# A triangle-update layer with a mixture of experts on one core: the second root ahead of the first logits, two PSUM banks dealt out anew, and two groups' weights turned before the second variance

## The reference, cut to what matters

```python
x = x + triangle(ln_c(x))         # x is (1, 128, 128, 32)
t = tokens(x)                     # 16384 tokens of 32 channels
t = t + moe(ln_t(t))

# triangle(Z)
z = layernorm(Z, ln1_w, ln1_b)
g = sigmoid(z @ gate_w.T + gate_b)
left, right = split((z @ lrp_w.T + lrp_b) * mask * g)
tri = einsum('bikc,bjkc->bijc', left, right)
go = sigmoid(tri @ og_w.T + og_b)
tri + go * (layernorm(tri, ln2_w, ln2_b) @ op_w.T + out_bias)

# moe(x): 8 experts, the best 2 of each token
probs = softmax(x @ router_w + router_b)
top_p, top_i = top_k(probs, 2);  top_p = top_p / sum(top_p)
out = sum over the two of top_p * (x @ expert_w[e] + expert_b[e])
```

## Time and profile before

| | us |
|---|---|
| median of 3 runs | 144.69 (143.39 to 145.44) |
| the profiled execution, its own time | 144.41 |
| its span | 142.6 |
| PE busy in the span | 123.1 (86%) |
| DVE busy | 103.6 (73%) |
| ACT busy | 76.9 (54%) |
| POOL busy | 75.7 (53%) |

### The profile page before, as it was taken

How to read it: one execution, slowest core, us unless ns; L and a number is a source line. 1 busy time by engine, 2 the same in 40 slices (tenths; PEclk the granted TensorE clock), 3 DMA queues, 4 the chain that set the end, 5 groups by cost and what they waited for, 6 DMA issues and landing times. The chain is left out here.

```text
span 142.6 us, 2140 instructions
## 1 busy us (share of the span) xinstructions
PE 123.1 (86%) x708; PEld 53.8 (38%) x711; DVE 103.6 (73%) x173; ACT 76.9 (54%) x136; POOL 75.7 (53%) x73
## 2 busy tenths in 40 slices
PE   5999788999999699889799899695899669989970
PEld 2425145767679565344134443123121111212210
DVE  0096948787774699999918994462978995989951
ACT  4168473565413359898853349858256454474400
POOL 6001033799900089989930173063552974869970
PEclk9999999999999999999999999999559996999999
DMA  4997000000000000000000899987188978871112
GB/s 90 321 350 320 0 0 5 0 0 2 0 5 0 0 2 0 0 5 0 0 0 9 186 208 205 210 187 170 26 202 202 215 182 197 199 283 74 74 74 78
DMA packets 6171, 14.55 MB, mean 102 GB/s; under 512 B 1392, under 2 KB 1648, under 8 KB 6160
## 3 DMA queue, kind: packets, MB, share of 16 engines
q1 hardware_dynamic: 6160, 14.41, 38.1%
HBM read 3.85 MB, written 2.10 MB: 42 GB/s over the span
## 5 line engine op out<-in xcount | busy, mean ns | idle before, releaser
L429 POOL TENSOR_TENSOR work<-work,late_sb 128x512 f32<-128x512 f32 x12 | 15.0, 1274 | 9.7 <-ACT work L526 9.7
L627 ACT ACTIVATE wcopy<-ps 128x512 f32<-128x512 f32 x24 | 13.6, 597 | 9.1 <-PE ps L1024 9.0
L791 PE MATMUL ps<-w1m,xk 64*128 64x256 f32 x128 | 16.2, 391 | 0.8 <-DVE xk L1103 0.3
L1024 PE MATMUL ps<-w3F,selb 32*128 32x512 bf16 x64 | 12.0, 412 | 4.0 <-DVE prod L1306 2.7
L441 POOL TENSOR_TENSOR work<-tri,stats 128x512 f32<-128x512 f32 x8 | 8.8, 1114 | 11.6 <-DVE stats L1172 11.4
L526 ACT ACTIVATE work<-ps 128x512 f32<-128x512 f32 x16 | 9.6, 597 | 9.0 <-PE ps L791 9.0
L491 POOL TENSOR_TENSOR prod<-wcopy,lr 128x512 f32<-128x512 f32 x6 | 8.3, 1405 | 11.3 <-ACT wcopy L627 8.6
L791 PEld LDWEIGHTS ps<-w1m,xk 64*128 64x128 f32 x128 | 11.6, 186 | 5.5 <-DVE lr L1118 2.4
L1118 DVE TENSOR_TENSOR lr<-ps,work 128x512 f32<-128x512 f32 x16 | 10.6, 687 | 2.5 <-POOL work L429 2.5
L1089 DVE TENSOR_SCALAR xk<-ps,head_sb 128x512 f32<-128x512 f32 x8 | 6.4, 798 | 7.4 <-ACT triF L510 7.2
L1024 PEld LDWEIGHTS ps<-w3F,selb 32*128 32x128 bf16 x64 | 3.0, 93 | 20.4 <-issue 6.6
(11 more groups left out here) (136 smaller groups left out, 257.2 us busy)
## 6 DMA issues: line engine op xcount, KB each, us to landing
lr<-triF SPq DMA_DIRECT2D x32, 128.0 KB, 2.3
xi<-in_x_F SPq DMA_DIRECT2D x8, 256.0 KB, 4.6
tri<-triF SPq DMA_DIRECT2D x16, 128.0 KB, 2.4
xk<-triF SPq DMA_DIRECT2D x16, 128.0 KB, 2.3
out<-xi SPq DMA_DIRECT2D x8, 256.0 KB, 2.1
late_sb<-in_late SPq DMA_DIRECT2D x1, 914.0 KB, 7.6
choice_sb<-in_choice SPq DMA_DIRECT2D x1, 336.5 KB, 7.8
early_sb<-in_early SPq DMA_DIRECT2D x1, 257.0 KB, 5.5
```

Source lines behind the costliest of these rows:

```text
L429: pool.tensor_tensor(unit_gates(u), unit_gates(u), mask[:, first_tokens(u)].unsqueeze(1).broadcast_to([P, 2 * C, 8]), ALU.mult).then_inc(s ...
L627: act.activation(wcopy[:, a * W:(a + 1) * W], ps[:, HELD + POOL_N[a] % 4, :], ACT.Copy)\
L791: m = pe.matmul(ps[:, unit_bank(u) + b, 2 * F1 * q:2 * F1 * (q + 1)], xk[rows, at:at + P], w1[rows, 2 * F1 * b:2 * F1 * (b + 1)], start=Tr ...
L1024: pe.matmul(ps[:, HELD + n % 4, :], selb[slot_rows(n % R), n * P:(n + 1) * P], col(w3F, g)[slot_rows(n % R), :], start=True, stop=True).th ...
```

## The change

Nothing is computed otherwise; instructions are put in another order on four engines, and two jobs get other PSUM banks.

- First half: `turn_root(1)` goes ahead of `logits(0)` on PE, and `spread_root(1)` ahead of `logit_bias(0)`. DVE does `tri_squares(4..7)` and `tri_root(1)` ahead of the copy of z3. `spread_root` now signals after each of its four matmuls, not after the last. All four `tri_scaled(4..7)` stand ahead of the compares.
- Last gate: `out_gate(7)` goes ahead of `update(6)` and `update(7)` on PE; in `RING` ("g", 7) moves behind ("z", 4). `round_part(0, 0)` goes ahead of the table load on ACT.
- `turn_weights(1, 2)` stands ahead of `variance(1)`, `turn_weights(3)` behind `turn_std(1)`. The spreads of groups 0, 1 and 2 move forward.
- First sums: ("y", 0) moves in `RING` ahead of ("p", 4). Both sums of group 0 stand ahead of `pair_differences(1)`; `sum_experts(1, 0)` goes ahead of `lead(1)`.
- DVE does all products of groups 0 and 1 and `add_x1(0)` ahead of the second half's compares, and `add_x1(1)` between `weigh(1)` and `remainder(1, 0)`. The copy of z7 goes from ACT to DVE. POOL does two products of group 1 ahead of `root_of_each(1)`.

```diff
-                ("g", 7), ("z", 4), ("z", 5), ("z", 6), ("z", 7), ("w", 0), ("var", 1), ("logit", 1), ("w", 1),
-                ("w", 2), ("w", 3), ("std", 1), ("p", 4), ("p", 5), ("p", 6), ("p", 7), ("wins", 1), ("back", 1),
-                ("lead", 1), ("y", 0), ("y", 1), ("w", 4), ("w", 5), ("y", 2), ("y", 3), ("w", 6), ("w", 7), ("y", 4),
+                ("z", 4), ("g", 7), ("z", 5), ("z", 6), ("z", 7), ("w", 0), ("w", 1), ("w", 2), ("w", 3), ("var", 1),
+                ("logit", 1), ("std", 1), ("y", 0), ("p", 4), ("p", 5), ("p", 6), ("p", 7), ("wins", 1), ("back", 1),
+                ("lead", 1), ("y", 1), ("w", 4), ("w", 5), ("y", 2), ("y", 3), ("w", 6), ("w", 7), ("y", 4),
...
-        X1_COPIED_BY_VECTOR = [1, 3, 5]
+        X1_COPIED_BY_VECTOR = [1, 3, 5, 7]
...
             out_gate(7)
+            round_part(0, 0)
             load_roots()
-            round_part(0, 0)
...
-                    m = pe.matmul(ps[:, HELD + g, :], lcp("slot")[slot_rows(g), :], rootF[h][slot_rows(g), :],
-                                  start=True, stop=True)
-                m.then_inc(s_rb, 1)
+                    pe.matmul(ps[:, HELD + g, :], lcp("slot")[slot_rows(g), :], rootF[h][slot_rows(g), :],
+                              start=True, stop=True).then_inc(s_rb, 1)
...
-                dve.wait_ge(s_rb, g // HG + 1)
+                dve.wait_ge(s_rb, g + 1)
...
             variance(0)
+            turn_root(1)
             logits(0)
-            turn_root(1)
+            spread_root(1)
             logit_bias(0)
-            spread_root(1)
...
             lead(0)
+            out_gate(7)
             update(6)
             update(7)
-            out_gate(7)
```

More of the change, by code:

```diff
@@ L494, in _ @@
             product(0, *POOL_N)
+            product(1, *POOL_N[0:2])
             root_of_each(1)
-            for g in range(1, G):
+            product(1, *POOL_N[2:3])
+            for g in range(2, G):
                 product(g, *POOL_N)
@@ L1053, in _ @@
             spread(0, 2, 3)
+            turn_weights(1, 2)
             variance(1)
+            spread(0, 4, 5, 6, 7)
             logits(1)
-            spread(0, 4, 5, 6, 7)
             logit_bias(1)
-            turn_weights(1, 2, 3)
-            turn_std(1)
             spread_first(1)
             spread(1, 2, 3)
+            turn_std(1)
+            turn_weights(3)
+            spread(1, 4, 5, 6, 7)
+            sum_experts(0, 0)
+            sum_experts(0, 1)
             pair_differences(1)
-            spread(1, 4, 5, 6, 7)
+            spread_first(2)
+            spread(2, 2, 3)
             turn_root_back(1)
             wins(1)
-            sum_experts(0, 0)
+            sum_experts(1, 0)
             lead(1)
-            sum_experts(0, 1)
-            for g in range(2, G):
+            spread(2, 4, 5, 6, 7)
+            sum_experts(1, 1)
+            for g in range(3, G):
                 spread_first(g)
@@ L1252, in _ @@
             closed(3)
-            tri_squares(4)
-            tri_squares(5)
+            for g in range(4, G):
+                tri_squares(g)
             x1_copy(1)
-            tri_squares(6)
-            tri_squares(7)
+            tri_root(1)
             x1_copy(3)
-            tri_root(1)
             def compared(n):
@@ L1312, in add_x1 @@
                 dve.tensor_tensor(col(xi, g), ring_bank(("y", g)), col(xi, g), ALU.add).then_inc(s_yf, 1)
-            tri_scaled(4)
-            tri_scaled(5)
+            for g in range(4, G):
+                tri_scaled(g)
             for n in range(HG):
@@ L1318, in _ @@
             x1_root(0)
-            tri_scaled(6)
+            gated_update(4)
             top_two(0)
-            tri_scaled(7)
-            gated_update(4)
+            gated_update(5)
             lead_scaled(0)
             top_two_roots(0)
-            gated_update(5)
+            gated_update(6)
             weigh(0)
-            gated_update(6)
+            gated_update(7)
             remainder(0, 0)
-            gated_update(7)
+            closed(7)
             remainder(0, 1)
-            closed(7)
             x1_copy(5)
-            product(0, *VECTOR_N)
-            product(1, *VECTOR_N[0:2])
+            product(0, VECTOR_N[0])
+            x1_copy(7)
+            product(0, *VECTOR_N[1:5])
+            product(1, *VECTOR_N)
             x1_root(1)
+            add_x1(0)
             for n in range(HG, G):
                 compared(n)
-            product(1, VECTOR_N[2])
             top_two(1)
-            product(1, *VECTOR_N[3:5])
+            product(2, *VECTOR_N[0:2])
             lead_scaled(1)
             top_two_roots(1)
-            add_x1(0)
+            product(2, VECTOR_N[2])
             weigh(1)
-            product(2, *VECTOR_N[0:2])
+            add_x1(1)
+            product(2, VECTOR_N[3])
             remainder(1, 0)
-            product(2, *VECTOR_N[2:4])
+            product(2, VECTOR_N[4])
+            product(3, VECTOR_N[0])
             remainder(1, 1)
-            product(2, VECTOR_N[4])
-            add_x1(1)
-            product(3, *VECTOR_N)
+            product(3, *VECTOR_N[1:5])
             add_x1(2)
```

11 lines of the change are left out of this document (5 added, 6 removed).

## The result

The changed kernel takes 149.19 us (median of 4 runs, 147.71 to 150.13) against 144.24 us, a ratio of 1.032 with an interval of 1.025 to 1.038. It is 3.2% slower. Ratios and intervals here leave out runs over 1.5% above the quickest of the same kernel, so that 1.032 lies a little under 149.19/144.24. The forecast was 146.2 us, at most 148.6.

What follows compares the result with a forecast made beforehand. The end was taken to move with the turn of group 4's weights (116.18 us, 28.2 us following), not PE's 86%. Terms 0 + 0.65 + 0.75 + 0.4 = +1.8 us on 144.41 gave 146.2, range 142.8 to 148.6.

Steps and rivals of the forecast that it cites:

- the clock there: Around group 0's sums and the second half's pair differences: one sum at the low clock, +0.75 us (0 to 2.3).
- the second dip: Low clock after 116.9 us, 3.4 us long: left as it is, since PE is as empty before 117 in both.
- Second root, last gate: First half, up to group 0's first spreads: all edits sum to 0 us, between -0.2 and +0.5.
- Weights ahead of the variance: Second half's router from the spreads at 91.95: logits copy 0.9 us earlier, turn_std(1) at 98.05 instead of 98.48, -0.4.
- Sums ahead of the differences: After turn_std(1): pair differences +3.55 us, their fourth waiting for add_x1(0), lead(1) at 107.65, +0.65 at full clock.
- From lead to the turned weights: From lead(1) to the turn of weights 4 and 5: 9.55 us instead of 9.17, +0.4 (ends 9.2 and 10.5).
- The fixed train: Groups 3 to 7 after the turned weights of group 4: same instructions and order in both kernels, 28.2 us.
- rival A: Group 0's sums and the pair differences, 100.8 to 107: low clock back in full, +4.3 us, 148.7; chance 0.28.
- B: Clock holds throughout, the pause before 117 also short enough: terms +0.65, 0, +0.4, -0.35, 144.1 us; chance 0.18.
- C: Groups 0 to 2 out of the way, DVE and POOL reach group 3 earlier, waits go: about 142 us; chance 0.12.

Runs made afterwards that it cites:

- e4: The kernel before with only the first half's parts, root and gate: 144.78 us, ratio 1.001 (0.996 to 1.005).
- e3: The kernel before with only the weights part, turn_weights(1, 2) ahead of variance(1), their banks and the copy of z7: 144.48 us, ratio 1.001.
- e5: The changed kernel with 26 PE matmuls of ones, results unread, in four of PE's waits: 145.17 us against 144.04, quotient of medians 1.008.
- e9: The kernel before with filler matmuls of ones only where PE has nothing to do: 142.70 us against 144.67, ratio 0.990 (0.979 to 1.000).
- e2: The kernel before with only the sums part of the change: 148.47 us against 144.85, ratio 1.027 (1.020 to 1.034).
- e7: The changed kernel with add_x1(1) behind the second remainder on DVE: 147.58 us against 144.04, 2.5% over.
- e12: The changed kernel once more, nothing altered, on another chip: 148.36 us against 144.67, ratio 1.023 (1.011 to 1.035).
- e11: The changed kernel with three pair differences ahead of group 0's sums and x1_root(1) back behind two products of group 1: 148.82 us, ratio 1.027.
- e6: The kernel before with fillers before turn_std(1) and three behind each of group 3's first four spreads: 145.78 us against 144.04.
- e10: The changed kernel with the edits of e5 and e7 together: 144.66 us against 144.67, ratio 1.002 (0.999 to 1.005).

## Why the prediction was wrong

The sign and the order of events were right, the size was not: +1.8 us forecast, +4.6 us measured (3.2% of 144.24). The step that failed is the clock, in two places: the term "the clock there", for which I took one sum at the low level, 0.75 us, and the second dip, which I left "as it is" at no cost because "PE is as empty before 117 in both". By the steps:

- **Second root, last gate.** Forecast 0, between -0.2 and +0.5. The turn of group 0's weights came at 90.52 against 90.4 forecast, and e4 gives a ratio of 1.001. Right, and so were the single moves (spread of the root 1 us earlier, differences near 75.8, update 6 at 83.38 against 83.25).
- **Weights ahead of the variance.** Forecast `turn_std(1)` at 98.05, measured 98.23; e3: no difference. Right.
- **Sums ahead of the differences.** Forecast +3.55 us at the differences and +0.65 us at `lead(1)` at full clock. In e5, at full clock, the differences start at 103.14 (102.85 forecast) and `lead(1)` at 108.07 (107.65). The term is right as a time, 0.4 us short. It hides what the order costs, because it sets the new order at full clock against an old kernel that was itself slowed: against e9, with the clock full in both, the order costs 2.75 us at `lead(1)`. I had written that part of it was a clock given back, and then booked only a small piece of the clock again. The term also names the wait of the fourth difference for `add_x1(0)`; that wait exists and costs nothing, since the compares start late and run on without a gap.
- **The clock there.** Forecast 0.75. Measured in the profiled execution: both sums in the low stretch, 3.23 us instead of the 1.92 of e5, +1.3, and `lead(1)` 1.38 us behind that of e5 (109.45 against 108.07). In e2, e7 and e12, where the stretch was longer, the sums took 3.64 us and the differences 1.95 to 2.10 instead of 1.57: +2.1 to +2.3, which is rival A's price for this place. How often that happens cannot be said, since the other executions have no trace.
- **From lead to the turned weights.** Forecast 9.2 to 10.5, taken 9.55; measured 9.26 here and 9.27 in e5. Right, and e7 shows that 1.34 us of it is the wait for `add_x1(1)`. The first remainder took 1.03 - 0.68 = 0.35 us longer than the second, beside POOL products, instead of the 1.1 of the earlier trace rows; the second took the plain 0.68.
- **The fixed train.** Forecast 28.2 us, measured 147.71 - 118.71 = 29.0. At full clock it takes 27.3 us in both orders (e5, e9), so the second dip costs the old order 0.9 us and the new one 1.7. The instructions are the same; the low clock lasted over more of them. Of the two stretches just ahead of the second dip, the first of the kernel before, the other of the changed one, PE had work in 1.70 of 3.5 us and in 2.09 of 3.8 us:

```profile
113.50:117.00 3.50, 1.70 (x14) 0.61 (x18) 3.50 (x7) 2.34 (x4) 2.75 (x3) 1.00 0.80 184
110.50:114.30 3.80, 2.09 (x14) 0.44 (x13) 2.98 (x6) 2.23 (x4) 1.76 (x1) 1.00 0.93 207
```

So PE was about as empty in both, as I wrote, but the new order has the thin stretch earlier and the clock low from 114.3, not from 117.0, to 124.5, not 120.4. I had compared the emptiness and not the length of what follows.

For the profiled executions this closes: +2.4 us at `lead(1)`, +0.1 from there to the turned weights, +0.8 behind them, +3.3 in all (147.71 - 144.41), against +1.4, +0.4 and 0 in the forecast. That is 1.5 us of the miss. The rest is the distance from the quickest run to the median, which has no trace.

At the medians: e9 is 2.0 us under the kernel before, which is what the dips cost the old order. For the new order it is 1.032 - 1.008 = 2.4%, 3.5 us, from runs on two chips. The order itself costs 2.9 us (e5 against e9). 2.9 + 3.5 - 2.0 = 4.4 us, against 4.6 measured. This is a split and no independent check, since e5 and e9 stand in for the two orders at full clock and the terms between them must come out near the whole. With e12's 2.3% in place of 3.2% the dips of the new order would cost 2.2 us. Either way the order is the greater part, and the clock adds 0.2 to 1.5 us net, because the old order pays for its dips too.

Of the rivals, A comes nearest, with 148.7 us worked out for it and 149.19 measured; I gave it 0.28. The closeness is partly luck: 0.95 of A's +4.3 us was to come from remainders beside POOL, which did not happen, A had nothing for the longer second dip, and in the profiled execution the low clock ended at 104.1, not near 107. B's condition was made true in e5, and gave 145.17, not 144.1: `lead(1)` came 0.4 us later than B had it, and the full clock took 0.9 us off the train, not 1.4. C did not come. With groups 0 and 1 done earlier, DVE still waited for PE, since `turn_weights(4, 5)` stands ahead in PE's list. DVE of the changed kernel:

```profile
122.68 1.89 DVE L1310 TENSOR_TENSOR work<-ps,lr 128x512 f32<-128x512 f32 x3 [4.09 <-PE ps L1024]
```

Why the clock fell for longer is only half settled. Ahead of the turned weights PE's spreads come one by one, each behind a DVE product, and with fillers there and at the other three places of e5 the clock stays full. What share each gap has was not tried.

## What to carry to other kernels

Compare two orders at the same clock: if the kernel at hand has a low stretch on its critical chain, a new order that shows little loss against its trace may be slower by all that the old one had lost to the clock, and will then pay for its own dip on top. When work is moved ahead on one engine, follow it through the lists of the others: here the sums stood ahead of the differences on PE and their addition ahead of all four compares on DVE, and taking back the first alone (e11) gained next to nothing. Cheap filler matmuls in a true wait are worth trying, but not between an instruction on the path and its successor (e6), and they have to be placed anew when the wait gets shorter (e10).

## What the runs showed of the hardware

- In these two traces the lower clock began each time after a stretch in which PE had work about half of the time, with no single wait over 1.7 us: 1.44 us of 3.1 and 1.70 of 3.5 before, 1.96 of 3.8 and 2.09 of 3.8 after. It was then held though PE was busy nearly all the time (3.40 us of 3.4, 3.29 of 3.5). The Trainium skill (TensorE: Matmul & The Clock Gate, Part 1: The HAM clock gate) says that the clock is gated by how busy PE has been recently, and that there are two levels. The rows agree: 0.50 or 0.51, or 0.99 or 1.00, in every stretch that lies on one side.
- How long it stays low varies from run to run with the same order: both sums of group 0 took 3.23 us in the profile of the changed kernel and 3.64 in those of e7 and e12. With PE kept busy (e10, granted clock 1.000 in every run) ten runs lay within 0.6 us, beside 2.2 us for those of the old kernel without its longest. That the clock is the main cause of the scatter is likely from this, not shown: two runs of the changed kernel with mean clocks of 0.950 and 0.954 had spans of 145.9 and 147.3 us.
- Three bfloat16 fillers of 512 columns add 0.75 us at the high level (e5) and 1.4 us at the low one (e6): a filler that arrives too late to hold the clock costs nearly double.
